# Rows of x loaded as 128-byte blocks and turned in 32x32 squares by VectorE, in place of TensorE

## The reference

```
x = x + L0(x, lengths, ...)      # y = causal convolution of x*mask with K[head], + D*x, times mask
x = x + L1(x, languages, ...)    # x @ W.T + 2 * sum_e gate_e * (x @ A_e.T) @ B_e.T
# L1: logits = x @ Wr.T + 5 * onehot(language); softmax of the best two; their gates
```

## Time and profile before

| | |
|---|---|
| median of 3 runs | 664.79 us (664.57 to 667.07) |
| the profiled execution's own time | 665.17 us |
| its span, first to last instruction | 663.4 us |
| PE busy | 641.9 us, 97% |
| DVE busy | 491.8 us, 74% |
| ACT busy | 462.5 us, 70% |
| mean busy share of the 16 DMA engines in an odd and an even step | 0.25 |
| granted clock of PE, mean | 0.992 |

### The profile page before, as it was taken

How to read it: one execution, slowest core, us unless ns; L and a number is a source line. 1 busy time by engine, 2 the same in 40 slices (tenths; PEclk the granted TensorE clock), 3 DMA queues, 4 the chain that set the end, 5 groups by cost and what they waited for, 6 DMA issues and landing times.

```text
span 663.4 us, 12421 instructions
## 1 busy us (share of the span) xinstructions
PE 641.9 (97%) x3663; PEld 616.3 (93%) x3663; DVE 491.8 (74%) x1504; ACT 462.5 (70%) x977; POOL 35.1 (5%) x61
## 2 busy tenths in 40 slices
PE   4798999999999999999999999999999999999997
PEld 4697989999999999999999999999999999999997
DVE  7888687777778777777877777787777778776741
ACT  5788788586776858686686868678676867864531
POOL 2241000000000000000000000000000000000000
PEclk9798999999999999999999999999999999999999
DMA  6531313333312132322213223211333321122212
GB/s 186 151 104 32 82 39 66 72 71 71 68 36 59 50 71 71 71 71 46 57 40 71 71 71 71 59 45 39 71 71 71 71 67 39 42 66 41 41 33 63
DMA packets 24064, 43.40 MB, mean 65 GB/s; under 512 B 9928, under 2 KB 14832, under 8 KB 24048
## 3 DMA queue, kind: packets, MB, share of 16 engines
q1 hardware_dynamic: 19168, 27.37, 17.9%
q10 hardware_dynamic: 4880, 15.83, 9.6%
HBM read 26.35 MB, written 16.85 MB: 65 GB/s over the span
## 4 chain that ended last, share of the span: by engine, by line
PE 91%; ACT 4%; DVE 3%; issue 1%; DMA 0%; ACTq 0%; SPq 0%; DVEq 0%
PE pmg L1269 58%; PE pc L1208 13%; PE pmg L1256 7%; PE px L1208 5%; PE px L1201 4%; PE pmg L1250 1%; DVE state L935 1%; PE pmg L1279 1%; PE pmg L1167 1%; ACT swapped L531 1%; PE pmg L1177 1%; DVE w_lo L867 0%; DMA logs<-in_L_cond_log_A_real 0%; ACT y_hi L558 0%; ACT z_swap L480 0%
## 5 line engine op out<-in xcount | busy, mean ns | idle before, releaser
L1269 PE MATMUL pmg<-w_hi,y_hi 128*128 128x384 f32 (+1 forms) x768 | 265.7, 346 | 0.7 <-DVE y_lo L982 0.7
L1269 PE MATMUL pmg<-w_hi,y_lo 128*128 128x384 f32 (+1 forms) x768 | 259.8, 338 | 0.0
L1269 PE MATMUL pmg<-w_lo,y_hi 128*128 128x384 f32 (+1 forms) x768 | 259.7, 338 | 0.0
L1269 PEld LDWEIGHTS pmg<-w_hi,y_hi 128*128 128x128 f32 x768 | 144.3, 188 | 1.7 <-issue 1.1
L1269 PEld LDWEIGHTS pmg<-w_hi,y_lo 128*128 128x128 f32 x768 | 144.4, 188 | 0.5
L1269 PEld LDWEIGHTS pmg<-w_lo,y_hi 128*128 128x128 f32 x768 | 144.3, 188 | 0.0
L531 ACT ACTIVATE swapped<-state 64x128 f32<-64x128 f32 x192 | 59.4, 309 | 65.4 <-DVE state L935 64.0
L935 DVE SCALAR_TENSOR_TENSOR state<-swapped,scan_tab,state 128x192 f32<-128x192 f32 (+1 forms) x240 | 73.8, 349 | 15.6 <-ACT swapped L531 11.1
L576 ACT ACTIVATE result<-pmg 128x384 f32<-128x384 f32 (+1 forms) x96 | 41.7, 448 | 39.4 <-PE pmg L1256 37.1
L964 DVE TENSOR_TENSOR s_lo<-state,s_hi 128x896 fp32r<-128x896 f32 x31 | 33.9, 1093 | 30.0 <-ACT s_hi L553 30.0
L982 DVE TENSOR_TENSOR y_lo<-xt,y_hi 128x1024 fp32r<-128x1024 f32 x32 | 39.2, 1225 | 20.6 <-ACT y_hi L558 19.2
(11 more groups left out here) (206 smaller groups left out, 1112.0 us busy)
## 6 DMA issues: line engine op xcount, KB each, us to landing
rows<-in_x SPq DMA_DIRECT2D x64, 256.0 KB, 5.3
out<-result ACTq DMA_DIRECT2D x60, 256.0 KB, 4.0
toe<-kpad SPq DMA_DIRECT2D x30, 128.0 KB, 5.1
rows<-in_L_cond_W SPq DMA_DIRECT2D x3, 512.0 KB, 6.9
result<-in_L_cond_W SPq DMA_DIRECT2D x3, 512.0 KB, 5.9
w_rows<-in_L_cond_W SPq DMA_DIRECT2D x2, 512.0 KB, 4.5
result<-in_L_cond_A SPq DMA_DIRECT2D x1, 512.0 KB, 6.2
b_rows<-in_L_cond_B SPq DMA_DIRECT2D x2, 256.0 KB, 6.7
```

Of the source, the lines that this page charges most:

```text
L1269: ins = nc.tensor.matmul(pm[:, n, 0:o1 - o0], y[s][:, c, :], w[:, c, o0:o1], start=(c == 0 and y is y_hi and w is w_hi), stop=(c == CH - 1 ...
```

## The change

From pair 4 on, PE no longer turns rows. SP loads a pair in eight transfers, one for each quarter k of a 128-sample chunk and each half d of the sequences: 32 sequences by 16 pieces of 32 samples (128 bytes). They land so that quarter k lies in partitions 32k to 32k + 31. DVE then needs only to turn 32x32 squares, which it does with two `transpose` instructions of 128 partitions by 512 elements straight from `rows` to `xt`. ACT makes `u_hi` from `xt` and no longer copies `px` to `xt`. The two waits that `turn_rows` did on PE before it wrote `px` now stand in `control`. SP waits for DVE's turn (`xt_ready`) in place of PE's before it loads into a buffer again.

```diff
+            def load_blocks(b, m):
+                i, s = 2 * b + m, m % 2
+                for k in range(P // SQUARE):
+                    for d in range(SEQS // SQUARE):
+                        sp.dma_start(
+                            rows[s][k * SQUARE:(k + 1) * SQUARE, d * HALF:(d + 1) * HALF].rearrange(
+                                "p (n l) -> p n l", l=SQUARE),
+                            bass.AP(x.tensor, 2 * i * LEN + k * SQUARE + d * (SQUARE * HEADS * LEN),
+                                    [[HEADS * LEN, SQUARE], [P, 2 * CH], [1, SQUARE]])
+                        ).then_inc(rows_in[s], 16)
...
             def step(b, m, rows_left=True):       # SP
                 if rows_left:
-                    sp.wait_ge(px_full, 2 * b + m + 3)
-                    load_rows(b, m + 4)
+                    sp.wait_ge(xt_ready, 2 * b + m + 3)
+                    load_blocks(b, m + 4)
...
+            def split_turned(b, m):               # ACT, in place of split_rows
+                i, s = 2 * b + m, m % 2
+                act.wait_ge(xt_ready, i + 1)
+                act.wait_ge(conv_done, i - 1)
+                nc.scalar.activation(u_hi[s][:, :, :], xt[s][:, :, :], ACT.Copy).then_inc(uhi_ready, 1)
...
+            def turn_rows(b, m):                  # DVE
+                i, s = 2 * b + m, m % 2
+                dve.wait_ge(rows_in[s], TURNED_BY_PE + BLOCK_LOADS * (b + m // 2 - 1))
+                dve.wait_ge(ylo_ready, i - 1)
+                for d in range(SEQS // SQUARE):
+                    turned = xt[s][:, :, :].rearrange("p c (h d b) -> p h c d b", h=2, b=SQUARE)[:, :, :, d, :]
+                    blocks = rows[s][:, d * HALF:(d + 1) * HALF].rearrange("p (h c l) -> p h c l", h=2, l=SQUARE)
+                    ins = vec.transpose(turned, blocks)
+                ins.then_inc(xt_ready, 1)
...
+                if ahead:                         # DVE's step, between the scan and split_states
+                    turn_rows(b, m + 3)
+                if rows_left:
                     split_states(b, m + 2)
...
+                if alone:                         # PE, control
+                    pe.wait_ge(v_copied, i)
+                    pe.wait_ge(scan, SCAN * (i - 1) + 1)
...
-                project(b, m, 2, 0, 7)            # PE's step
-                if ahead:
-                    turn_rows(b, m + 3)
-                project(b, m, 2, 7, 8)
+                project(b, m, 2)
```

More of the change, by code:

```diff
@@ L37 @@
 DUOS = HEADS // DUO
+SQUARE, HALF = 32, LEN // 2
 MAGIC = 1.5 * 2.0 ** 23
@@ L237, in cond_resid_kernel @@
         START = 16
+        TURNED_BY_PE = 64
+        BLOCK_LOADS = 16 * 8
         ROUTER = 9
@@ L334, in _ @@
             sp.wait_ge(px_full, 3)
-            load_rows(0, 4)
+            load_blocks(0, 4)
             sp.wait_ge(pm_free, 6)
@@ L344, in step @@
                 if rows_left:
-                    sp.wait_ge(px_full, 2 * b + m + 3)
-                    load_rows(b, m + 4)
+                    sp.wait_ge(xt_ready, 2 * b + m + 3)
+                    load_blocks(b, m + 4)
                 store_kernel(b, m + 3)
                 load_toe(b, m + 3)
-            step(0, 1)
+            sp.wait_ge(px_full, 4)
+            load_blocks(0, 5)
+            step(0, 1, rows_left=False)
             with sp.Fori(1, LOOPS) as b:
@@ L692, in step @@
                 if rows_left:
-                    split_rows(b, m + 2)
+                    split_turned(b, m + 2)
                 ratios(b, m)
@@ L1104, in _, with step @@
                 pass
+            turn_rows(0, 4)
             split_states(0, 3)
-            def step(b, m, rows_left=True, kernels=True):
+            def step(b, m, rows_left=True, kernels=True, ahead=True):
                 split_toe(b, m + 1)
@@ L1133, in _ @@
             step(LOOPS, 0, kernels=False)
-            step(LOOPS, 1, kernels=False)
-            step(LOOPS + 1, 0, rows_left=False, kernels=False)
+            step(LOOPS, 1, kernels=False, ahead=False)
+            step(LOOPS + 1, 0, rows_left=False, kernels=False, ahead=False)
             route(LOOPS + 1, 1)
@@ L1232, in convolve, with control @@
                 ins.then_inc(conv_done, 1)
-            def control(b, m):
+            def control(b, m, alone=False):
                 i, s = 2 * b + m, m % 2
+                if alone:
+                    pe.wait_ge(v_copied, i)
+                    pe.wait_ge(scan, SCAN * (i - 1) + 1)
                 pe.wait_ge(uhi_ready, i + 1)
@@ L1364, in _, with step @@
             add_lora(BANK_ORDER[2])
-            turn_rows(0, 4)
-            def step(b, m, rows_left=True, ahead=True):
+            def step(b, m, rows_left=True):
                 if rows_left:
@@ L1376, in step @@
                 if rows_left:
-                    control(b, m + 2)
-                project(b, m, 2, 0, 7)
-                if ahead:
-                    turn_rows(b, m + 3)
-                project(b, m, 2, 7, 8)
+                    control(b, m + 2, alone=True)
+                project(b, m, 2)
                 add_lora(BANK_ORDER[2])
@@ L1387, in _ @@
             step(LOOPS, 0)
-            step(LOOPS, 1, ahead=False)
-            step(LOOPS + 1, 0, rows_left=False, ahead=False)
+            step(LOOPS, 1)
+            step(LOOPS + 1, 0, rows_left=False)
             wait_y(LOOPS + 1, 1)
```

## The result

The changed kernel took 660.41 us (median of 7 runs, 659.9 to 661.51); the kernel before took 665.75 beside it (7 runs). The ratio is 0.9919, 95% interval 0.9902 to 0.9936. A second series, further down, gave 0.9935 (0.9912 to 0.9958). The profiled executions took 665.17 and 660.82 us, 4.35 apart; their spans are 663.4 and 659.0. So of 24.6 us taken off TensorE (PE) about 4 to 5 came off the time.

What follows compares the result with a forecast made beforehand. PE and a DVE-ACT ring were taken to bound the loop together. A pair of steps: -0.21 + 0.10 - 0.25 + 2 x 0.23 = +0.10 us, +1.3 over 13 pairs; +1.6 in all, 666.4 us, range 660 to 685.

Steps and rivals of the forecast that it cites:

- The likeliest case: Whole kernel, transposes together taking 1.20 to 1.65 us: +1.6 us forecast, 660 to 673 us, 60 in 100.
- Two engines bound the loop; PE's 24.6 us turn into waiting: Loop: PE's saved 24.6 us become waits for `gated`, about 0.5 us in even and 1.0 in odd steps.
- the ring: DVE and ACT's loop chain, convolution through scan, `s_hi`, `s_lo`, `route` and `gated` to next convolution; claimed to bound beside PE.
- ACT's freed copy gives 0.25 in even steps: Even steps: without ACT's 1.02 us copy, `half_sum` no longer waits for `ratio`; 0.25 us gained.
- Even steps give back 0.21 at the gates: Even steps, gates' end to convolution's second matmul: 0.98 us becomes the idle PE's 0.77, 0.21 gained.
- Odd steps lose 0.10 there: Odd steps, gates' end to convolution's second matmul: 0.67 us becomes 0.77, as the load is no longer readied early.
- D: Time of DVE's two transposes between scan and `s_lo`: taken as 1.43 us, making `s_lo` 0.23 late each step.
- The turn ahead of the loop and the steps behind it, +0.3: Outside the loop: DVE's 0.23 us paid ahead of it, where PE wins nothing; about 0.1 added in the first step behind.
- The transfers are hidden: SP's queue: eight issues, 4096 pieces a pair, at most 9.8 us within 15.8 before the next store; priced at nothing.
- Two passes over float32 squares: Rival at DVE's transposes: 2.44 us for two, `s_lo` 1.24 late, kernel at 695 us; 11 in 100.
- To scale a short transpose by its columns: Skill page's 311 ns taken per 128 columns: 2.49 us a pair, kernel near 696; not followed, no separate chance.
- Short transposes, at 660: Rival at DVE's transposes: both together at or below 1.20 us, `s_lo` not late, -4.7 us, 660; 8 in 100.

Runs made afterwards that it cites:

- A second series: The changed kernel measured again, unaltered, against the kernel before, beside the run with transposes ahead of the scan: 659.97 us, ratio 0.9935.
- small transposes: Changed kernel with each of DVE's two transposes turning only 32 of its 512 columns: 658.25 us, 0.9897 of the kernel before.
- doubled transposes: Changed kernel with every pair turned a second time into an unused buffer, ahead of the real turn: 699.65 us, 1.054 of the kernel before.
- Z moved late in both kernels: DVE's powers (0.6 us, odd steps) moved behind `route`, ACT's swap behind `gt_hi`: 651.76 us in the changed kernel, 663.27 in the one before.
- the experiment: Changed kernel with ACT's former copy of 1024 elements put back ahead of `u_hi`, into an unused buffer: 664.61 us, 0.9993 of the kernel before.
- the early ones: Changed kernel with DVE's two transposes moved from behind the scan to ahead of it, behind `y_lo`: 687.37 us, 1.0345 of the kernel before.

## Why the prediction was wrong

The mechanism was right and the sign was not. The likeliest case was +1.6 us and "no change"; measured were -4 to -5, clear of noise. That 660.41 still lies within the wide range of 660 to 685, at its edge, is luck.

- *Two engines bound the loop; PE's 24.6 us turn into waiting.* Right. PE's load waits 20.5 us in 26 steps (I had said near 20), about 1.0 in odd steps. The small and the doubled transposes, and Z moved late in both kernels, show the ring to be the bound. In even steps the load waits 0.35 where I had said 0.5. Two signs were less than forecast: PE's busy time fell by 16.6 and not by 25, ACT's by 21.3 and not by 28.
- *ACT's freed copy gives 0.25 in even steps.* Right: 0.24 in the rows, 0.29 a pair in the experiment.
- *Even steps give back 0.21 at the gates.* Right: 329.53 - 328.75 = 0.78, where it was 0.98.
- *Odd steps lose 0.10 there.* Wrong: 310.78 - 310.11 = 0.67, as before. I had put the idle case of the loop's first step, an even one, on odd steps. 0.10 a pair.
- *D, the length of the two transposes.* This is the step that failed. I took 1.43, over the nearest row, by choice; it is 1.29. `s_lo` is 0.12 late and not 0.23, 0.22 a pair. In addition `s_lo` itself runs 0.97 to the start of `t_lo` where it took 1.01, 0.08 a pair; where it waits again, with the small transposes and with the early ones, it takes 1.01 again. Together with the odd steps 0.40, against the 0.38 between the forecast's +0.10 and the measured -0.28. Over the twelve pairs measured it is 4.5 of the 6 us by which I missed. D alone is 2.9 us in 13 pairs, enough to turn the sign of the sum, but not to carry it past the 3.3 us that I called no change. The nearest row taken as it stood, 1.35, would have said -0.06 a pair.
- *The turn ahead of the loop and the steps behind it, +0.3.* Wrong in sign. The loop's first step is 0.42 longer, but what lies behind its last odd step is 1.20 shorter. There I had priced only DVE's delay and not what PE, 0.88 earlier, gives. In the first two steps behind the loop the convolution's second matmul came 0.99 and 0.93 behind the gates and now comes 0.58 behind them, 0.76 of the 1.20. What shortens the rest was not tried.
- *The transfers are hidden.* Nothing speaks against it, but it isn't shown by a run of its own. The terms read from the rows, -0.20 and -0.24 in even steps, +0.24 and -0.08 for `s_lo`, add up to -0.28 a pair, as measured, and leave nothing for 4096 pieces.
- *The rivals.* Two passes over float32 squares: no, 687 ns for 512 columns is close to the predicated copy's 735. To scale a short transpose by its columns is wrong as well: two of 32 columns took 0.30 together, and two of 512 took 1.29, so most of the short one is fixed. The page "VectorE: DVE Perf Modes" of the Trainium skill, "The three transpose paths", gives 311 ns for 128x128 in bf16, and the estimate of 2.49 came from scaling it in that way; no run here has that shape. Short transposes, at 660, was the rival whose number came out, though not by its mechanism: `s_lo` is late after all.

A sum of terms of 0.1 to 0.3 us with both signs can't be called to 0.1 by reading alone, and 13 to 28 repetitions make each 0.1 worth 1.3 to 2.8 us. Everything except D and the odd steps' 0.10 was read from the rows it belonged to. With the nearest row for D the sum for the whole kernel would have been near -0.5 us, still what I called no change; a gain beyond that needed a shorter D, odd steps that lose nothing, and the steps behind the loop, which I had not worked out.

## What to carry to other kernels

Where the waiting of the busiest engine for another is no longer than a hop, taking work from it frees little (here 0.2 of 0.88 us, in every second step of the loop); look instead at what stands on the other engine between its last wait and the signal. Put work that must be added into a wait of that engine's chain (here it cost 0.09 us there, and 0.86 more ahead of the scan), and move out of the chain what isn't needed for the signal: here moving Z and `t_lo` behind `route` was worth 14 us with the turns gone from PE. Of the two only Z was tried in the kernel before, and was worth 1 to 2 us there. Price an operation without a row by the nearest row, and don't add to it.

## What the hardware showed that I had not expected

The more PE waited, the more often its granted clock fell. Read in windows of 1 us over the loop, it stayed at 1.00 in every version in which PE's longest noted wait for `gated` in the loop was 1.1 us or less, the changed kernel and the one of before among them. With every pair turned twice PE waits 1.95 us in odd steps and 1.2 in even ones, and the clock fell at five places of the loop. One of them in the windows view (length, busy time and count of PE, PEld, DVE, ACT and POOL, then the clock, DMA share, GB/s):

```profile
242.00:243.00 1.00, 0.00 (x0) 0.00 (x0) 0.89 (x5) 0.99 (x2) 0.00 (x0) 1.00 0.27 61
243.00:246.40 3.40, 2.96 (x8) 2.31 (x9) 1.62 (x3) 1.46 (x6) 0.00 (x0) 0.58 0.88 168
```

PE did nothing for the microsecond from 242 to 243, and in the stretch behind it, to 246.4, the mean granted clock is 0.58, so most of that stretch ran at the lower level of 1.2 GHz. Most waits of this length were not followed by a fall; what decides it is not shown. The price can be read from two neighbouring pairs of steps of that run, each from the end of `gated` in an odd step to the next:

```profile
529.79:571.86 42.07, 38.89 (x204) 36.66 (x204) 33.81 (x99) 26.86 (x58) 1.42 (x2) 0.96 0.32 56
571.86:612.34 40.48, 37.32 (x204) 35.47 (x204) 33.80 (x99) 26.86 (x58) 1.42 (x2) 1.00 0.33 58
```

The pair with a fall in it takes 1.6 us more. Five of them are some 8 us, an estimate, of the 39 that this version lost. With the transposes early PE waits 1.65 in odd steps, and the clock fell once in the loop:

```profile
359.77:401.00 41.23, 38.88 (x204) 36.79 (x204) 31.62 (x95) 26.53 (x58) 0.40 (x2) 0.96 0.32 57
401.00:440.89 39.89, 37.31 (x204) 35.48 (x204) 31.63 (x94) 26.64 (x58) 1.42 (x2) 1.00 0.34 59
```
